# Attention stage of a gated cross-attention block on one core: VectorE's round reordered, later norms of x on ScalarE, maxima and the last chunk's halves moved

## What is computed

```
x = x + tanh(g_xattn) * xattn(layernorm(x), ctx)      # x: 4 x 1024 x 256, ctx: 4 x 154 x 256
x = x + tanh(g_ffn)   * ffn(layernorm(x))             # 256 -> 768 -> 256, gated, quantised as below

def xattn(hc, hq):                                    # hc = layernorm(x), hq = ctx
    Sim  = hc@w1 + hq@w2 + (hc*w3)@hq.T + b           # [1024, 154] for each of the 4 batches
    A    = softmax(Sim, axis=2);  hq_hat = A @ hq
    Batt = softmax(max(Sim, axis=2), axis=1)          # one weight per row of x
    hc_bar = Batt @ hc                                # one vector per batch
    return concat([hc, hq_hat, hc*hq_hat, hc*hc_bar]) @ W_qv + b_qv
```

## Time and profile before

| what | value |
|---|---|
| median of 3 runs | 476.89 us (476.28 to 477.19) |
| profiled execution, its own time | 476.41 us |
| its span | 474.6 us |
| its mean granted TensorE clock | 0.968 |
| busy in it: PE, DVE, ACT, POOL | 444.3, 363.1, 265.9, 111.2 us |

### The profile page before, as it was taken

One profiled execution on the slowest core, in us unless ns is written; L12 is line 12 of the kernel. 1 busy time (PEld: TensorE's weight loads), 2 busy tenths in 40 slices (PEclk: granted clock), 3 DMA queues, 4 the chain that ended last, 5 costly groups with the idle time before them and its releaser, 6 DMA issues.

```text
span 474.6 us, 6752 instructions
## 1 busy us (share of the span) xinstructions
PE 444.3 (94%) x2432; PEld 304.9 (64%) x2432; DVE 363.1 (77%) x657; ACT 265.9 (56%) x325; POOL 111.2 (23%) x109
## 2 busy tenths in 40 slices
PE   4889999899899969969999999999999999799997
PEld 3777899789788858824444444444444444588886
DVE  6656888688858785658453579999998888898874
ACT  2667135523542513128333389999387768888760
POOL 1239137443735382100000003343100000000000
PEclk9999999799959988979999999999999999999999
DMA  8930002000200020020000000000000000344442
GB/s 243 319 135 0 1 2 89 1 0 1 90 0 1 0 90 0 1 88 0 0 0 0 1 1 0 0 0 0 1 1 0 0 0 0 101 125 134 149 136 68
DMA packets 20672, 21.13 MB, mean 45 GB/s; under 512 B 825, under 2 KB 20392, under 8 KB 20648
## 3 DMA queue, kind: packets, MB, share of 16 engines
q1 hardware_dynamic: 20628, 20.82, 13.9%
q10 hardware_dynamic: 20, 0.00, 0.0%
...
## 4 chain that ended last, share of the span: by engine, by line
PE 39%; DVE 26%; issue 20%; ACT 10%; POOL 2%; DMA 1%; ACTq 0%; POOLq 0%; DVEq 0%
PE ps L752 12%; PE ps L717 9%; PE ps L722 4%; DVE cols L1357 4%; PE ps L584 2%; DVE hid L1373 2%; DVE st L1110 2%; DVE h L1066 2%; DVE xa L1106 2%; ACT sc L822 2%; DVE st L1050 2%; ACT hid L960 2%; PE ps L539 2%; DVE yb L1123 1%; ACT sc L831 1%
## 5 line engine op out<-in xcount | busy, mean ns | idle before, releaser
L717 PE MATMUL ps<-xh,wuh 128*128 128x512 f16 x192 | 72.8, 379 | 1.1 <-DVE gq L1396 1.1
L717 PE MATMUL ps<-xh,wul 128*128 128x512 f16 x192 | 72.8, 379 | 0.0
L722 PE MATMUL ps<-xl,wuh 128*128 128x512 f16 x192 | 57.1, 379 | 0.0
L1336 DVE TENSOR_REDUCE cols<-hid x10 | 22.9, 2286 | 24.8 <-ACT hid L937 24.8
L752 PE MATMUL ps<-wdh,oh 128*128 128x256 f16 x168 | 37.4, 273 | 0.0
L752 PE MATMUL ps<-wdl,oh 128*128 128x256 f16 x168 | 37.4, 273 | 0.0
L717 PE MATMUL ps<-xh,wgh 128*128 128x512 f16 x96 | 36.4, 379 | 0.0
L717 PE MATMUL ps<-xh,wgl 128*128 128x512 f16 x96 | 36.4, 379 | 0.0
L937 ACT ACTIVATE hid<-ps 128x2048 f32 x10 | 18.8, 1875 | 28.0 <-PE ps L722 28.0
L539 PE MATMUL ps<-aT,cx 77*128 77x256 f32 x128 | 34.2, 415 | 0.2 <-ACT hqT L845 0.2
L717 PEld LDWEIGHTS ps<-xh,wuh 128*128 (+1 forms) x192 | 18.8, 98 | 24.3 <-issue 2.0
...
## 6 DMA issues: line engine op xcount, KB each, us to landing
...
```

Of the source, the lines that this page charges most:

```text
L717: pe.matmul(ps[hf][:, q, :], w_[:, d, ds(k * P, P)], xh[:, d, n], start=d == 0 and w_ is wh, stop=False)
L722: mm = pe.matmul(ps[hf][:, q, :], wh[:, d, ds(k * P, P)], xl[:, d, n], start=False, stop=d == KD - 1)
L1336: dve.tensor_reduce(gmx[:, ds(k * 2 + hf, 1)], unit(hid, k, hf), AX.X, ALU.max, apply_absolute_value=True).then_inc(gm_done, 1)
```

## The change

1. **VectorE's round.** `attended` leads the slot, and is now that of tile m-4. `stats` stands between `scored` and `normed`, `norm_x1` behind `normed`, `max_y` behind it. Where s = 3, the norm of x1 and its maximum go to the start of the next slot. `weight_unit` stands at the slot's end.
2. **Norms of x.** h of tiles 8 to 15 is made by ScalarE (Identity with scale rstd and bias -mean * rstd). VectorE makes the bias for two rows' columns at once (`row_shift`). h_rdy is split into hv_rdy and ha_norm_rdy. ScalarE's `attended` goes ahead of its `normed`.
3. **Maxima.** From the second batch on, TensorE's `batch_max` is issued between the two halves of `project`; `weight_max` goes to the slot's end.
4. **The weights.** W_AT = [10, 14, 17]; `weight_scales` one slot ahead of W_AT, `weight_q` in it and in the next, `weight_values`, `weight_f` and `weight_n` two slots after it. All nine transposes are done by slot 21, and the ninth `weight_part` waits until the scale of y is known.
5. **GpSimd.** `row_weigh` goes ahead of `y_std`; its last addition (`row_pair`) stays behind it.
6. **The last tile.** VectorE does the statistics of both halves first, then norm and maximum of each. TensorE's warming matmuls are dealt out anew (7, 2, 2, 10 for 10, 4, 9), and the second half's transposes use another bank. The first chunk is quantised in two halves (`xqi0_rdy`, `xh0_rdy`).

```diff
-        W_AT = [10, 14, 18]
+        W_AT = [10, 14, 17]
+        NF = 2 * NP
-        TURN_AT = {17: (0,), 18: (1,), 19: (2, 3), 20: (4, 5), 21: (6, 7), 22: (8,)}
+        TURN_AT = {17: (0,), 19: (1, 2), 20: (3, 4, 5), 21: (6, 7, 8)}
...
@@ scalar, in the loop over m
+                if NF <= m + 1 < N and s < 3:
+                    norm_x(m + 1)
                 if 2 <= m <= N + 1:
                     turned_a(m - 2)
                 if 1 <= m <= N:
                     exps(m - 1)
+                if NF <= m + 1 < N and s == 3:
+                    norm_x(m + 1)
+                if 3 <= m <= N + 2:
+                    attended(m - 3)
+                if 1 <= m <= N:
                     normed(m - 1)
...
@@ vector
+            def row_shift(n):
+                b, s, par = place_of(n)
+                dve.wait_ge(rstd_rdy, n + 1)
+                q = slice(par * TB + 2 * s, par * TB + 2 * s + 2)
+                dve.scalar_tensor_tensor(nmr[:, q], mv[:, par, 2 * s:2 * s + 2, 0], -1.0, rstd[:, q], ALU.mult, ALU.mult).then_inc(nmr_rdy, 1)
...
@@ vector, the loop over m as it is now
                if 4 <= m <= N + 3: attended(m - 4)
                if 3 <= m and m + 1 < NF: norm_x(m + 1)
                if NF <= m + 1 < N: row_shift(m + 1)
                if s == 0 and 1 <= b < B: context_bias(b)
                if s == 1 and 1 < b <= B: batch_shift(b - 1)
                if s == 0 and LAG < m: norm_x1(m - LAG - 1); max_y(m - LAG - 1)
                if LAG <= m and not late: residual(m - LAG)
                if 1 <= m <= N: scored(m - 1)
                if s == 0 and 1 <= b <= B: batch_max(b - 1)
                if 1 <= m and m + 3 < N: stats(m + 3)
                if 1 <= m <= N: normed(m - 1)
                if s == 1 and b == 1: batch_shift(b - 1)
                if LAG <= m and not late: norm_x1(m - LAG)
                if s == 3 and 1 <= b <= B: summary(b - 1)
                if LAG <= m and not late: max_y(m - LAG)
                for i in range(3):
                    if m == W_AT[i] - 1: weight_scales(i)
                    if m == W_AT[i]: weight_unit(i)
                    if m == W_AT[i] + 2: weight_values(i)
                if LAG <= m and late: residual(m - LAG)
```

181 lines of the change are left out of this document (107 added, 74 removed).

## The result

| what | before | after |
|---|---|---|
| median | 476.75 us (476.28 to 477.19, 4 runs) | 464.87 us (461.44 to 465.64, 4 runs) |
| profiled execution, its span | 476.41, 474.6 us | 465.64, 463.8 us |
| mean granted clock | 0.968 | 0.982 |
| forecast | | 453.7 us (449.0 to 462.0) |

The ratio is 0.975, 95% interval [0.9725, 0.9771]: 11.9 us faster, where 23.2 were forecast. The sign was right, the size half, and the time lies 2.9 us above the range.

What follows compares the result with a forecast made beforehand. TensorE was taken to lose time to waits for a late VectorE and the clock falls behind them, and in the last chunk. Terms 12.6 + 3.8 + 0 + 6.8 = 23.2 us gave 453.7 us, range 449 to 462.

Steps and rivals of the forecast that it cites:

- slots 16 to 19: Attention's slots 16 to 19: a new wait of weight_scales(2) replaces the old loss, 0 us, between gain 4 and loss 6.
- The gated part: Behind the attention stage: from 213.57 us on nothing changes.
- the signs of being right: prT without idle; clock 1.00 in slots 8 to 15; predicted waits in place; first hidden matmul some 23 us earlier.
- none of being wrong: Signs against: any fall of the clock in slots 8 to 15, or a wait on the new ScalarE norm.
- The waits of slots 11 and 15: Slots 11 and 15: TensorE's waits for turn_a go, with their clock: 12.6 us gained, bounds 0 and 12.6.
- The fill: 12.00 to 48.32 us: slots 5 and 6 no longer loop through VectorE's hqT wait; 3.8 us gained, bounds 0 to 4.5.
- by that rule the held pairs don't leave with this change: VectorE two-port instructions and GpSimd's exclude each other for a whole instruction, so norm_x1 still meets row_add.
- a rival on slots 11 and 15: VectorE still late in slot 11 or 15; 5.2 to 7.4 us missing, 459 to 461 us; chance 0.12.
- The first rival: Slot 16's new wait costs more: TensorE loses 3 to 6 us more in slots 17 to 20; 457 to 460; chance 0.18.
- The last chunk: 201.21 to 213.57 us: second half's statistics to diagonal and warming matmuls run sooner; 6.8 us gained, between 3.5 and 7.5.
- The ScalarE norm: Eight pairs of h moved to ScalarE: 0.5 us per instruction; VectorE's row_shift estimated 0.2, at most 0.9.
- The fourth rival: ScalarE's norm comes late and turn_h waits in slots 8 to 15: slower, 478.8 us; chance 0.03.

Runs made afterwards that it cites:

- Item 10: The changed kernel with W_AT = [9, 13, 17] in place of [10, 14, 17] and nothing else: 457.61 us, ratio 0.960.
- item 7: Items 6 kernel with GpSimd kept quiet beside VectorE's norms of x1 in slots 17 and 18, bias_x(14) and bias_x(15) moved to slot 19's end: 456.62 us, ratio 0.959.
- item 2: The changed kernel with block scales of its own for the third weight, so weight_scales(2) needn't wait for weight_n(1): 461.48 us, ratio 0.970.
- Items 6: The changed kernel with own block scales for the third weight, row_add(3) ahead of y_std(11), and 32 warming matmuls for 22 before the down product: 459.52 us, ratio 0.964.
- item 4: The kernel before with the change's new last tile alone, including the ninth weight part and the first chunk in halves: 469.95 us, ratio 0.988.
- Item 3: The changed kernel with 32 instead of 22 warming matmuls ahead of the down product: 463.11 us, ratio 0.973.
- item 15: The changed kernel with all 16 norms of x on VectorE, none on ScalarE: 468.48 us, ratio 0.984.
- items 13: The kernel before with attended(m-4) at the head of VectorE's round, in place of attended(m-3) in its middle: 468.16 us, ratio 0.985.
- item 12: The changed kernel with W_AT = [9, 13, 17], row_add(3) ahead, 32 warming matmuls, GpSimd quiet in slots 17 and 18, summary(3) ahead of attended(15): 448.81 us, ratio 0.942.

## Why the prediction came out half right

Three of the four terms were too large, and slots 16 to 19, put at nothing, cost most; each of the four came inside its own bounds, all on the low side. The gated part, put at nothing because no work changes there, lost 2.2. All the signs of being right were seen but one (the first hidden matmul came 13.0 us earlier, not 23), and none of being wrong: they told of the mechanism, and only the last of the size.

**The waits of slots 11 and 15, 12.6 us forecast, 10.3 measured.** The mechanism held: prT's idle time went from 15.9 to 1.6 us, the reciprocal is early, the clock is 1.00. One reading of before was short: of slot 11's 1.76 us only 0.56 is turn_a's. The larger wait, behind which the clock fell, is that of batch_cols (L622) for ScalarE's copy of cxT (L864):

```profile
84.41 0.66 PE L529 MATMUL ps<-ident,sc 128*77 128x128 f32 x4 [0.56 <-ACT sc L831]
86.27 0.86 PE L622 MATMUL ps<-ones,h 128*128 128x1 f32 x4 [1.20 <-ACT cxT L864]
```

That copy stands behind L831 on ScalarE, which then works without a gap from 83.62 on, so it goes back to the same late reciprocal. What was mis-sized is "nothing more is lost there": 1.00 and 0.88 us of waiting are left, not for turn_a but for hc and we, the next in line. Item 10 shows what they come from: W_AT = [9, 13, 17] alone removes both, so it is the weights' steps, a slot too late; which of them was not separated. The prediction looked for the slack of the reciprocal only, and not for that of summary in the same slot.

**The fill, 3.8 forecast, 1.9 measured.** Slots 5 and 6 were to take 3.9 and 3.7 us in place of 10.7; they took 4.1 and 4.8 (27.69 to 31.82 to 36.58). Slot 6 is the one that was mis-sized: VectorE's pair for h ahead of it (29.13) took 2.64 us, where the walk had 0.9, the scores came behind it, and turn_a waits 0.68 us for ScalarE's scaled exps. Slot 7 came as forecast, we waits 0.61. GpSimd's bias_x stands beside that pair (28.83, 2.79 us), as in the cases of item 7; taking it away was not tried.

**Slots 16 to 19, 0 forecast, -5.6 measured.** This is the step that failed. Every member of its chain came true, and in its order, but late by an amount that grew: values done at 13.3 (forecast 11.0), weight_n 17.6 (15.4), weight_scales 20.6 (18.3), residual(11) and its statistics done at 32.2 (28.5), row sums ready at 36.4 (32.6), we at 41.2 (36.3), slot 20 at 46.5 (40.5). The 2.3 us at the first step lie where VectorE is held three times beside GpSimd's weight_q and bias_x: norm pairs of 1.88 (131.72) and 1.62 (138.34) in place of 0.73, and the diagonal of 1.34 (137.00) in place of 0.29. The next 1.4 lie where a norm pair takes 2.84 beside row_pair and weight_q; the 1.1 before we is ready are the pair of 2.69, the prT of 2.01 and the we of 2.44 beside row_add, weight_q and bias_x; and the last 1.1 are the clock of 0.50 behind the wait of 3.05. The walk had taken each at 0.73 and 0.88, their undisturbed length, though the earlier trace rows showed a held pair of 2.22, and the trace of before has held ones in these very slots (pairs of 1.69 at 152.51 and 2.58 at 169.26, a we of 2.08 at 175.29). The sentence "by that rule the held pairs don't leave with this change" was right, but it went only into a rival on slots 11 and 15, not into this walk, the one place with all the GpSimd work of a batch and two weights. The first rival had the size, 3 to 6 us, but by the wait of slot 16 and the clock, not by held instructions. That wait is 2.0 us of it by the columns (item 2), the held pairs of slots 17 and 18 with the moved bias_x are 3.05 (item 7), and the old slots of the weights, which remove the wait as well, 4.15 (item 10); these three overlap and don't add up.

The Trainium skill (SBUF — State Buffer, Who interferes with whom) says that VectorE in a two-port mode and GpSimd exclude each other for a whole instruction, and that an instruction of VectorE with two inputs in SBUF contends too, with one of GpSimd that reads SBUF. Items 6 and 7 agree for the first (0.73 against 2.84), and the prT of 2.01 beside bias_x for the second. By that page a TENSOR_REDUCE is never held, and the trace agrees: L1200 at 164.01 takes 0.69 us with GpSimd at work all the while, as it does elsewhere.

**The last chunk, 6.8 forecast, 6.1 to 6.5 measured.** The chain came as written: second half's x1 at 194.47, diagonal at 197.70, ten warming matmuls in 2.3 us at clock 1.00. It is the one term that stood alone, and item 4 gives it alone.

**The gated part, "nothing changes", -2.2 measured.** No work changed, but the clock fell before the down product, on a wait that had left it alone before. The prediction had counted the falls only in the part it looked at. Item 3 shows the term and, in the profiled execution, removes it (260.4); whether an execution pays it is chance as far as these traces tell.

**The ScalarE norm.** Estimated 0.5 us, it took 0.588 in the mean; row_shift, estimated 0.2 and at most 0.9, took 0.552. The move is worth 3.6 to 4.6 us (item 15, by medians and by ratios), at one place that the prediction had not named. The fourth rival, by which it would come late, did not happen.

Together: 12.6 + 3.8 + 0 + 6.8 was forecast; 10.3 + 0.3 + 1.9 - 5.6 + 6.1 - 2.2 = 10.8 came in the spans. Two parts alone, items 13 and 4, add to 14.8 us; the whole change gives 11.9. Item 10 shows the largest thing taken back: with the weights' scales and values in the slots that they had before, the changed kernel is 7 us faster.

**What stays open.** The gap between 463.8 and 459.6 us of span among executions of the same kernel was not traced. Of the 3.2 us of span that item 12 gains, 1.1 lie in slots 16 to 19 up to we and 2.4 behind it, with 0.3 lost in the fill; which of the later ones come from the clock alone was not separated. What makes TensorE's clock fall behind one wait and not behind a longer one stays open too.
